# Moving an MLP out of the last tiles into the wait behind the last chunk

## What is computed

```
x0 = xk = e                                   # (b, 39, 16)
for W in (f0, f1, f2):
    z = einsum('bfd,bgd->bfgd', x0, xk).reshape(b, f*g, d)
    xk = einsum('bpd,pm->bmd', z, W);  outs.append(xk)
z = sum(concatenate(outs, axis=1), axis=-1)   # (b, 384)
h = relu(concatenate([z, dense_ctx], axis=1) @ W_top1 + b_top1)
h = relu(h @ W_top2 + b_top2)
y = h @ W_top3                                # (b, 1)
```

## Time and profile before

| | us |
|---|---|
| median of 3 runs | 1350.27 |
| lowest and highest | 1345.81, 1350.93 |
| the profiled execution | 1340.59 |
| its span | 1338.9 |
| TensorE busy in it | 1274.2 |
| VectorE, ScalarE, GpSimd busy | 1079.9, 1050.2, 662.8 |

### The profile page before, as it was taken

One profiled execution on the slowest core, in us unless ns is written; L12 is line 12 of the kernel. 1 busy time (PEld: TensorE's weight loads), 2 busy tenths in 40 slices (PEclk: granted clock), 3 DMA queues, 4 the chain that ended last, 5 costly groups with the idle time before them and its releaser, 6 DMA issues. The chain is left out here.

```text
span 1338.9 us, 21410 instructions
## 1 busy us (share of the span) xinstructions
PE 1274.2 (95%) x6680; PEld 979.7 (73%) x6680; DVE 1079.9 (81%) x2285; ACT 1050.2 (78%) x3363; POOL 662.8 (50%) x634
## 2 busy tenths in 40 slices
PE   1389999999999999999999999999999999999998
PEld 0357777777787777777777777777777777777787
DVE  2059989988889888788878888898887888788884
ACT  2058888888888888788878888888887888788884
POOL 7787556654545557454466545455474532233100
PEclk8689999999999999999999999999999999999999
DMA  5073022100311013110211103111031102110000
GB/s 142 11 196 98 21 58 67 52 28 3 104 33 38 28 29 88 44 32 14 73 51 51 29 3 98 32 44 29 20 90 50 31 13 70 49 49 27 1 1 1
DMA packets 51177, 63.60 MB, mean 48 GB/s; under 512 B 13067, under 2 KB 24344, under 8 KB 51019
## 3 DMA queue, kind: packets, MB, share of 16 engines
q1 hardware_dynamic: 34544, 56.08, 13.7%
q0 software_dynamic: 10128, 2.98, 2.1%
q10 hardware_dynamic: 6392, 3.18, 0.9%
HBM read 11.08 MB, written 1.02 MB: 9 GB/s over the span
## 5 line engine op out<-in xcount | busy, mean ns | idle before, releaser
L538 ACT ACTIVATE scaled_x<-Y,x_col 128x128 f32<-128x128 f32 x3072 | 929.8, 506 | 190.4 <-PE Y L844 178.8
L842 PE MATMUL Y<-f_high,cur_high 128*128 128x512 f32 (+1 forms) x1280 | 603.9, 472 | 3.7 <-DVE sum_b L688 2.0
L844 PE MATMUL Y<-f_high,cur_low 128*128 128x512 f32 (+1 forms) x1280 | 499.1, 390 | 0.0
L843 PE MATMUL Y<-f_low,cur_high 128*128 128x512 f32 (+1 forms) x1280 | 499.0, 390 | 0.0
L427 POOL TENSOR_TENSOR pairs<-shifted,base 117x512 f32<-117x512 f32 x186 | 241.8, 1302 | 435.9 <-PE C L770 434.0
L688 DVE SCALAR_TENSOR_TENSOR sum_a<-Y,x_col,sum_a 128x128 f32<-128x128 f32 x768 | 264.8, 345 | 155.6 <-PE Y L844 153.4
L391 POOL DMA_INDIRECT rows<-in_tbl_dram,ids_sb x312 | 306.6, 983 | 77.5 <-issue 65.9
L842 PEld LDWEIGHTS Y<-f_high,cur_high 128*128 128x128 f32 x1280 | 241.3, 189 | 95.8 <-issue 37.2
L843 PEld LDWEIGHTS Y<-f_low,cur_high 128*128 128x128 f32 x1280 | 242.2, 189 | 86.2 <-issue 52.1
L707 DVE TENSOR_REDUCE cur<-scaled_x 128x128 f32<-128x1920 f32 x128 | 275.6, 2153 | 15.0 <-ACT scaled_x L538 1.6
L844 PEld LDWEIGHTS Y<-f_high,cur_low 128*128 128x128 f32 x1280 | 240.7, 188 | 51.1
(11 more groups left out here) (90 smaller groups left out, 730.6 us busy)
## 6 DMA issues: line engine op xcount, KB each, us to landing
shifted<-x_seq SPq DMA_DIRECT2D x157, 234.0 KB
base<-x_seq SPq DMA_DIRECT2D x95, 78.0 KB
rows<-in_tbl_dram,ids_sb POOLq DMA_INDIRECT x312
shifted<-x_seq SPq DMA_DIRECT2D x31, 156.0 KB
G<-in_L_rec_f_dram ACTq DMA_DIRECT2D x3, 832.0 KB, 8.6
w_sb<-in_W_top_dram SPq DMA_DIRECT2D x1, 768.0 KB
f_ext<-in_L_rec_f_dram SPq DMA_DIRECT2D x1, 760.5 KB
w_sb<-in_W_top_dram SPq DMA_DIRECT2D x1, 512.0 KB
```

Source lines behind the costliest of these rows:

```text
L538: ins = act.activation(scaled_x[:, :, PLACE[c] + i], where[:, i * M:(i + 1) * M], ACT.Copy, scale=x_col[:, t // JT % QG, t % JT, f:f + 1])
L842: pe.matmul(where, ch, wh, start=True, stop=False)
L843: pe.matmul(where, ch, wl, start=False, stop=False)
L844: pe.matmul(where, cl, wh, start=False, stop=True).then_inc(y_filled, 1)
```

## The change

The MLP of part 6 leaves the loop. Its first layer goes behind the last chunk, into the bank of Y that held the G products `("G", NG - 1, 3)`, called `late`, ahead of the tail's first terms. Its second layer goes behind the G products of tile 127. Its third layer goes after 13 of the 39 fields of layer 2. The tail's fourth bank is this same bank, so its first two terms now come after layer 2. The other tail banks are one of the G banks and the banks of chunks 6 and 7 of tile 127. A new semaphore, `last_read`, counts ScalarE's three reads of the moved MLP. SyncE's store of `y_col` waits for it. In the loop, the MLPs of parts 0 to 5 are as they were, with the bank and the semaphore passed as arguments.

```diff
 def mlp_in_group(g):
     bt, q = divmod(g, QG)
-    if q == 0 and bt >= 2:
-        return bt - 2
-    return BT - 2 if g == NG - 1 else None
-
-def mlp_tile(g):
-    return 0 if g % QG == 0 else 2
+    return bt - 2 if q == 0 and bt >= 2 else None
...
+        late = y_bank(("G", NG - 1, 3))
         def tail_bank(m):
-            return (y_bank(("G", NG - 1, 2 + m)) if m < 2 else bank(NT - 1, 4 + m))[:, 0:P]
+            return (y_bank(("G", NG - 1, 2)), bank(NT - 1, 6), bank(NT - 1, 7), late)[m][:, 0:P]
...
-            sp.wait_ge(c_read, C_USE["mlp", BT - 2, 2] + 1)
+            sp.wait_ge(last_read, 3)
             sp.dma_start(out[0:B - P, :].rearrange("(t p) o -> p (t o)", p=P), y_col[:],
...
+            relu1(BT - 2, late, last_read)
             act.wait_ge(s_filled, S_USE["G", NG] + 1)
             read_g(NG, 0).then_inc(s_read, 1)
             read_g(NG, 2).then_inc(g_read, 1)
+            relu2(BT - 2, late, last_read)
+            read_y(BT - 2, late, last_read)
...
+            def tail_first(m):
                 tail1(m, w1_dense, z_dense[:, cols], True, False)
                 tail1(m, w1_sb[:, 0, :], z0[:, P * (bt % 3):P * (bt % 3 + 1)], False, False)
+
+            pe.wait_ge(g_read, 2 * NG)
+            pe.wait_ge(c_read, C_USE["l2", BT - 2, L2_PARTS - 1] + 1)
+            mlp1(BT - 2, range(4), late)
+            tail_first(0)
             pe.wait_ge(acc_steps, NST * t + FUSE[6] + 3)
+            tail_first(1)
             pe.wait_ge(scaled, NSC * t + SCALED.index(7) + 1)
-            for m in range(2, 4):
-                tail1(m, w1_dense, z_dense[:, cols], True, False)
-                tail1(m, w1_sb[:, 0, :], z0[:, P * (bt % 3):P * (bt % 3 + 1)], False, False)
+            tail_first(2)
             g_products(NG)
+            pe.wait_ge(last_read, 1)
+            mlp2(late)
             pe.wait_ge(c_read, C_USE["l2", bt, 0])
             pe.wait_ge(s_read, S_BEFORE["G", NG] + 1)
             pe.wait_ge(g_read, 2 * (NG + 1))
-            layer2(bt, range(NF), 0, NF)
+            layer2(bt, range(L2_F), 0, NF)
+            pe.wait_ge(last_read, 2)
+            mlp3(late)
+            layer2(bt, range(L2_F, NF), 0, NF)
+            pe.wait_ge(last_read, 3)
+            tail_first(3)
             for m in range(4):
                 tail1(m, w1_sb[:, 1, :], g_half(bt)[:, NF, :], False, False)
```

More of the change, by code:

```diff
@@ L108, in sum_bank_uses @@
         m = mlp_in_group(g)
-        stages = [("mlp", m, i) for i in range(3)] if m is not None else []
-        if q == 0:
-            uses += stages
+        if m is not None:
+            uses += [("mlp", m, i) for i in range(3)]
         if g:
             uses.append(("G", g - 1))
-        if q:
-            uses += stages
         if g + 1 < NG:
@@ L250, in build @@
         l2_filled = sem("l2_filled")
+        last_read = sem("last_read")
         m1_filled, m2_filled, m3_filled, y_ready = sem("m1_filled"), sem("m2_filled"), sem("m3_filled"), sem("y_ready")
@@ L540, in scale_chunk, with relu1, relu2, read_y @@
                 ins.then_inc(scaled, 1)
-            def relu1(bt, n):
-                act.wait_ge(m1_filled, n)
+            def relu1(bt, where, done):
+                act.wait_ge(m1_filled, bt + 1)
                 for m in range(4):
[L545 to L549, removed]
+                    ins = act.activation(h1[:, m, :], where[:, m * P:(m + 1) * P], ACT.Relu, bias=b1_sb[:, m:m + 1])
+                ins.then_inc(done, 1)
+            def relu2(bt, where, done):
+                act.wait_ge(m2_filled, bt + 1)
                 for m in range(2):
[L551 to L556, removed]
+                    ins = act.activation(h2[:, m, :], where[:, m * P:(m + 1) * P], ACT.Relu, bias=b2_sb[:, m:m + 1])
+                ins.then_inc(done, 1)
+            def read_y(bt, where, done):
+                act.wait_ge(m3_filled, bt + 1)
+                act.activation(y_col[:, bt:bt + 1], where[:, 0:1], ACT.Copy).then_inc(done, 1)
             read_scalars(0)
@@ L567, in _ @@
                     t = JT * g + j
-                    with_mlp = mlp is not None and j == mlp_tile(g)
+                    with_mlp = mlp is not None and j == 0
                     for c in range(CH):
@@ L577, in _ @@
                             if with_mlp:
-                                relu1(mlp, mlp + 1)
+                                relu1(mlp, C[:], c_read)
                         if c == AT_X:
@@ L582, in _ @@
                             if with_mlp:
-                                relu2(mlp, mlp + 1)
+                                relu2(mlp, C[:], c_read)
                         if g == NG - 1 and CH * j + c == AT_LAST_G - 2:
@@ L586, in _ @@
                     if with_mlp:
-                        read_y(mlp, mlp + 1)
+                        read_y(mlp, C[:], c_read)
                     if j == JT - 1 and g + 2 < NG:
                         read_scalars(g + 2)
+            relu1(BT - 2, late, last_read)
             act.wait_ge(s_filled, S_USE["G", NG] + 1)
@@ L808, in layer2, with mlp1 @@
                     ins.then_inc(l2_filled, 1)
-            def mlp1(bt, ms):
+            def mlp1(bt, ms, where):
                 cols = slice(P * bt, P * (bt + 1))
@@ L813, in mlp1, with mlp2, mlp3 @@
                     w = slice(m * P, (m + 1) * P)
[L814 to L817, removed]
+                    pe.matmul(where[:, w], w1_dense[:, w], z_dense[:, cols], start=True, stop=False)
+                    pe.matmul(where[:, w], w1_sb[:, 0, w], z0[:, P * (bt % 3):P * (bt % 3 + 1)], start=False, stop=False)
+                    pe.matmul(where[:, w], w1_sb[:, 1, w], g_half(bt)[:, NF, :], start=False, stop=False)
+                    ins = pe.matmul(where[:, w], w1_sb[:, 2, w], z2[:], start=False, stop=True)
                 if ms[-1] == 3:
                     ins.then_inc(m1_filled, 1)
-            def mlp2(bt):
+            def mlp2(where):
                 for m in range(2):
                     for k in range(4):
-                        ins = pe.matmul(C[:, m * P:(m + 1) * P], w2_sb[:, k, m * P:(m + 1) * P], h1[:, k, :],
+                        ins = pe.matmul(where[:, m * P:(m + 1) * P], w2_sb[:, k, m * P:(m + 1) * P], h1[:, k, :],
                                         start=k == 0, stop=k == 3)
                 ins.then_inc(m2_filled, 1)
-            def mlp3(bt):
+            def mlp3(where):
                 for k in range(2):
-                    ins = pe.matmul(C[:, 0:1], h2[:, k, :], w3_sb[:, k:k + 1], start=k == 0, stop=k == 1)
+                    ins = pe.matmul(where[:, 0:1], h2[:, k, :], w3_sb[:, k:k + 1], start=k == 0, stop=k == 1)
                 ins.then_inc(m3_filled, 1)
@@ L881, in _ @@
                         layer2(bt - 1, [L2_F * (q - 1) + f for f in L2_SLICES[s]], L2_F * (q - 1), L2_F * q)
-                    if mlp is not None and j == mlp_tile(g):
+                    if mlp is not None and j == 0:
                         if c == 0:
@@ L885, in _ @@
                         if c < 2:
-                            mlp1(mlp, (2 * c, 2 * c + 1))
+                            mlp1(mlp, (2 * c, 2 * c + 1), C[:])
                         if c == 5:
                             pe.wait_ge(c_read, C_USE["mlp", mlp, 1])
-                            mlp2(mlp)
+                            mlp2(C[:])
                         if c == 9:
                             pe.wait_ge(c_read, C_USE["mlp", mlp, 2])
-                            mlp3(mlp)
+                            mlp3(C[:])
                     if c == AT_X and q == 2 and bt + 1 < BT:
@@ L909, in tail1 @@
                 return pe.matmul(tail_bank(m), w[:, m * P:(m + 1) * P], z, start=start, stop=stop)
-            pe.wait_ge(g_read, 2 * NG)
-            for m in range(2):
+            def tail_first(m):
                 tail1(m, w1_dense, z_dense[:, cols], True, False)
                 tail1(m, w1_sb[:, 0, :], z0[:, P * (bt % 3):P * (bt % 3 + 1)], False, False)
+            pe.wait_ge(g_read, 2 * NG)
+            pe.wait_ge(c_read, C_USE["l2", BT - 2, L2_PARTS - 1] + 1)
+            mlp1(BT - 2, range(4), late)
+            tail_first(0)
             pe.wait_ge(acc_steps, NST * t + FUSE[6] + 3)
+            tail_first(1)
             pe.wait_ge(scaled, NSC * t + SCALED.index(7) + 1)
-            for m in range(2, 4):
-                tail1(m, w1_dense, z_dense[:, cols], True, False)
-                tail1(m, w1_sb[:, 0, :], z0[:, P * (bt % 3):P * (bt % 3 + 1)], False, False)
+            tail_first(2)
             g_products(NG)
+            pe.wait_ge(last_read, 1)
+            mlp2(late)
             pe.wait_ge(c_read, C_USE["l2", bt, 0])
```

## The result

The changed kernel took 1343.72 us (median of 21 runs, 1339.96 to 1348.70), the kernel before 1347.53 in the same comparison (21 runs, 1343.99 to 1353.85). The ratio is 0.9970, 95% interval 0.9957 to 0.9983: a gain of 3.8 us by the medians and, by the interval, between 2.3 and 5.8, inside the half per cent that the prediction calls no change. The sign was right and the size was about half.

What follows compares the result with a forecast made beforehand. The prediction took TensorE to set the pace in tile 126, then VectorE's chain, then TensorE again; -4.22 + 0.52 + 1.05 + 0.79 + 0.2 = -1.7 us, from 1350.27 to 1348.6 us, range 1342.5 to 1351.5.

Steps and rivals of the forecast that it cites:

- no change: Whole kernel: a time within 0.5%, 6.8 us, of the median; given a chance of 0.93.
- The sign: Whole kernel: the change was forecast to make it faster, by 1.7 us.
- The MLP leaves tile 126, VectorE closes its idles: Tile 126: without TensorE's MLP, VectorE's idles of 0.95, 0.27 and 2.76 us close; its path gets 4.22 us shorter.
- TensorE comes too late for the last G products: Behind the last chunk: moved work fills TensorE's 2.19 us idle and overruns it by 0.52 us; G products at 1318.60.
- The second layer costs 1.05 us beyond the wait it fills: Between last G products and layer 2: 1.19 us before becomes 2.24 us with the second layer, costing 1.05 us.
- Third layer and fourth pair, 0.79, and broken streams, 0.2: Within and behind layer 2: third layer 0.34 us and tail pair 0.45 us added in full, five stream breaks 0.2 us.
- The store of the seven columns costs nothing: End of kernel: the later output store finishes within 1.7 us, ahead of the last store, and costs nothing.
- The price of a record: TensorE's moved MLP: 111 ns per 128-column record, 5.68 us in all; at about 81 ns, 4.2 us.
- ScalarE's 24 steps: Tile 126: free at 1297.7, ScalarE needs 6.3 us, so scaling ends by about 1304.4, before the reduction at 1306.1.
- The step that fell short: Before the last G products: TensorE idles 2.19 us waiting for VectorE's last reduction, room for the moved work.
- The base: Whole kernel: the forecast gain was subtracted from the median of the runs shown, 1350.27 us, giving 1348.6 us.

Runs made afterwards that it cites:

- e6: Changed kernel with an MLP's products, unread, put back on TensorE in tile 126; tail (tile 125's last reduction to the end) 43.18 us, changed kernel 38.96.
- e7: Changed kernel with ScalarE's six ReLUs and the column copy put back into tile 126, no products; tail 39.01 us, changed kernel 38.96.
- e5: Changed kernel with the moved second layer behind 13 fields of layer 2 and the third behind 26; tail 39.84 us, changed kernel 38.96.
- e9: Kernel before with 9 unread products issued where TensorE idles 2.19 us for VectorE's last reduction; tail 40.69 us, ratio to before 0.9993.
- e10: Changed kernel without the MLP of part 6, with 11 unread products in TensorE's 2.71 us wait; tail 36.96 us, changed kernel 38.96.

## Why the prediction was right, and where it fell short

- **The MLP leaves tile 126, VectorE closes its idles:** 4.22 us forecast, 4.23 measured, and shown to be TensorE's stream by e6 and e7.
- **TensorE comes too late for the last G products:** 1318.60 forecast, 1318.69 measured.
- **The second layer costs 1.05 us beyond the wait it fills:** the start of the G products to layer 2 took 2.28 us (1322.76 to 1325.04), 2.24 forecast. e5 has the wait back at 0.74.
- **Third layer and fourth pair, 0.79, and broken streams, 0.2:** from the start of layer 2 to the issue of the last store 13.84 us passed before (1323.49 to 1337.33) and 14.66 after (1325.04 to 1339.70), 0.82 more where 0.99 had been forecast. So 0.17 too much stood here, and 0.13 too little in the two steps above (0.09 and 0.04). That the whole came out within 0.05 us, 1.66 against 1.70, is in part that the two cancel.
- **The store of the seven columns costs nothing:** it was issued at 1328.68 and the last one at 1339.70; no row waits for it.
- **The price of a record:** 111 ns held. Between 1323.15 and 1325.04, 16 records take 118 ns each with their start. The lower price, about 81 ns, that the Trainium skill gives in "TensorE: Matmul & The Clock Gate", section "Back-to-back issue gap", and the gain of 3 us estimated from it, were not seen in the tail.
- **A slip without effect:** ScalarE's 24 steps from 1297.7 end at 1304.0, where the prediction has 1304.4; the reduction that needs them began at 1306.12 (1310.19 - 4.07).
- **The step that fell short** is the first one: "TensorE's timeline has the other side: 2.19 us of idle". I priced that idle as idle only, by a profile in which it did no further harm. It has a second price, the clock of the 78 records behind it: nothing in the profile of before, 1.4 and 1.6 us in two others of the same order, and none in the three profiles of the changed kernel, which has no such idle. The Trainium skill, "TensorE: Matmul & The Clock Gate", section "HAM oscillation — how this bites in real kernels", tells how a wait between bursts of matmuls brings the lower clock back, on a kernel with longer waits. Here the clock fell behind shorter ones, of 2.2 and 2.7 us. I left the rule out, since one trace had 1.00 in all stretches that I read. The rows of before could only have shown the risk: TensorE's longest idle after the first 70 us, close before its longest unbroken run of small products.
- **The base:** three runs gave a median of 1350.27, 21 gave 1347.53. Of the 4.9 us between forecast and time, 2.7 are this. That the time lies in the stated range, 1342.5 to 1351.5, owes more to the width allowed for scatter than to the sum.

Open: whether the clock accounts for all that the schedule does not. By three profiles the two together give 0.998, and the first two ratios lie at 0.997. How often the clock falls in unprofiled executions is known only through the averages above.

## What to carry to other kernels

Here two engines alternated as the bound. Moving work from TensorE's busy stretch into its idle one gained what VectorE's chain got shorter, less what overflowed the idle. Both could be read off one trace to about a tenth of a microsecond, once single executions were compared from a common point inside the steady part. Price an idle of TensorE like the 2.2 us here twice: as idle, and as the clock of what follows. One profile didn't tell whether the clock falls there; take several, or fill the gap with products that nobody reads and see whether the rows behind it get shorter.

## What the runs showed of the hardware that was not expected

After 2.20 us of idle on TensorE, with 0.73 more soon after, the granted clock went to 0.50 in two profiles and stayed at 1.00 in the third, of the same order of work; by the end of an idle of 2.71 us it had fallen as well. In the first two it fell only after the longer idle had ended. Where the longest idle of TensorE in the tail was 0.9 us or less, in the eight profiles with the MLP of part 6 behind the last chunk and in e9 and e10, it never fell there. And the stretch from tile 4 to tile 125 repeats to 0.15 us in 1171 across all profiles; the scatter between profiles is made in the first 130 us.
